# Order of the work inside a state-space tile, and B's diagonal blocks in two buffers

## The reference, cut to what matters

```python
dlt, Bm, Cm = split(u @ Wdbc.T)                  # u is (T, E)
delta = softplus(dlt @ Wdt.T + bdt)              # (T, E)
dA  = exp(delta[..., None] * A)                  # A = -exp(Alog), (E, N)
dBu = delta[..., None] * Bm[:, None, :] * u[..., None]
h_t = dA_t * h_(t-1) + dBu_t                     # scan over time, for each (e, n)
y_t = sum_n h_t[e, n] * C_t[n] + u_t * Dp
out = ((act_mx * (y of s=0)) + (act_mx * (y of s=1))) @ Wf.T + bf + skip
```

## Time and profile before

| what | value |
|---|---|
| median of 3 runs | 6061.12 us |
| the profiled execution, its own time | 6069.96 us |
| its span, first to last instruction | 6068.1 us |
| mean granted TensorE clock | 0.977 of full |
| state-space part, first scan to last | 3098.9 to 6014.5 us |
| busy: PE, DVE, ACT, POOL | 5548.3, 4367.1, 2989.3, 2960.3 us |

### The profile page before, as it was taken

One profiled execution on the slowest core, in us unless ns is written; L12 is line 12 of the kernel. 1 busy time (PEld: TensorE's weight loads), 2 busy tenths in 40 slices (PEclk: granted clock), 3 DMA queues, 4 the chain that ended last, 5 costly groups with the idle time before them and its releaser, 6 DMA issues. The chain is left out here.

```text
span 6068.1 us, 136615 instructions
## 1 busy us (share of the span) xinstructions
PE 5548.3 (91%) x58510; PEld 3145.8 (52%) x58510; DVE 4367.1 (72%) x5872; ACT 2989.3 (49%) x4999; POOL 2960.3 (49%) x955
## 2 busy tenths in 40 slices
PE   8899979997989899859989899999999999999998
PEld 3455545553555555434445555555555555555555
DVE  1455545552655555546559999999999999999996
ACT  0122212221555555531256666666666666666664
POOL 0000000000000000014359989999898998989997
PEclk9999989998999999979999999999999999999999
DMA  6200020001000000014331111111111111201111
GB/s 222 70 31 31 23 74 32 31 23 63 10 17 17 17 17 17 8 58 156 129 110 49 61 39 48 51 58 65 49 50 39 56 65 49 68 25 54 63 47 31
DMA packets 145197, 321.73 MB, mean 53 GB/s; under 512 B 25946, under 2 KB 27227, under 8 KB 134379
## 3 DMA queue, kind: packets, MB, share of 16 engines
q1 hardware_dynamic: 142322, 309.20, 14.8%
q10 hardware_dynamic: 2304, 4.20, 0.2%
HBM read 238.46 MB, written 74.89 MB: 52 GB/s over the span
## 5 line engine op out<-in xcount | busy, mean ns | idle before, releaser
L1896 POOL TENSOR_TENSOR sc_state<-sc_state,sc_c_rows 128x2048 f32<-128x2048 f32 x512 | 2374.2, 4642 | 288.6 <-DVE sc_state L2203 275.4
L2203 DVE TENSOR_TENSOR_SCAN sc_state<-sc_decay,wide 128x512 f32<-128x512 f32 x2048 | 2346.7, 1200 | 101.7 <-PE wide L2062 97.3
L1987 ACT ACTIVATE sc_decay<-sc_delta,sc_neg_a 128x512 f32<-128x512 f32 x2048 | 1455.6, 720 | 817.4 <-DVE sc_state L2203 804.7
L2062 PEld LDWEIGHTS wide<-sc_diag,sc_du_t 64*64 64x64 f32 x32768 | 972.6, 133 | 692.2 <-issue 455.8
L2062 PE MATMUL wide<-sc_diag,sc_du_t 64*64 64x128 f32 x32768 | 1173.4, 273 | 140.3 <-DVE sc_state L2203 140.3
L2079 PE MATMUL wide<-sc_state,sc_half 64*64 64x512 f32 x8192 | 1077.3, 592 | 10.4 <-POOL sc_state L1896 10.4
L1377 DVE CUSTOM_DVE_ANT_0 l_prob<-wide,l_mask_add 128x512 f32<-128x512 f32 x512 | 340.0, 683 | 285.9 <-PE wide L1247 285.7
L2036 PE MATMUL wide<-sc_xn_t,sc_w_z 128*128 128x512 f32 x1024 | 509.9, 621 | 2.5 <-DMA sc_xn_t<-xn_d 2.5
L1162 ACT ACTIVATE l_prob<-l_prob,l_s_max 128x512 f32<-128x512 f32 x512 | 366.0, 716 | 229.3 <-DVE l_s_max L1377 228.9
L509 PE MATMUL wide<-l_w,l_xn_t 128*128 128x512 f32 x1024 | 445.1, 592 | 1.7 <-PEq L84 1.7
L1258 PE MATMUL wide<-l_ident,l_prob 128*128 128x128 f32 x2048 | 293.9, 281 | 65.7 <-DVE l_prob_t L1386 38.6
(11 more groups left out here) (202 smaller groups left out, 6547.7 us busy)
## 6 DMA issues: line engine op xcount, KB each, us to landing
sc_c_rows<-c_d SPq DMA_DIRECT2D x64, 1024.0 KB, 4.8
sc_w_z<-wz_tiles SPq DMA_DIRECT2D x128, 256.0 KB, 2.7
x<-l_out SPq DMA_DIRECT2D x24, 1024.0 KB, 4.2
l_x<-x SPq DMA_DIRECT2D x16, 1024.0 KB, 6.4
mx_d<-fr_mx SPq DMA_DIRECT2D x16, 1024.0 KB
sc_mx<-mx_d SPq DMA_DIRECT2D x64, 256.0 KB, 2.7
pro_w_mod<-in_mod_w SPq DMA_DIRECT2D x6, 2048.0 KB, 11.3
l_w<-in_att_w SPq DMA_DIRECT2D x12, 1024.0 KB, 12.5
```

Of the source, the lines that this page charges most:

```text
L1896: pool.tensor_tensor(state[quad % STATES][:, :, :], state[quad % STATES][:, :, :], c_rows[(r * 4 + q) % ROWS][:, :, :], ALU.mult).then_inc ...
L1987: act.activation(decay[step % DECAYS][:, :], delta[slot % 2][:, :], ACT.Exp, scale=neg_a[:, s, m, n:n + 1]).then_inc(decay_ready, 1)
L2062: last = pe.matmul(to[cols_to, k, :, :], du_t[slot % 2][rows, k, cols_to], diag[rows, c, k, :, :], start=True, stop=True)
L2203: dve.tensor_tensor_scan(state[quad % STATES][:, step % 4, order], decay[step % DECAYS][:, order], pair[:, i, order], 0.0, ALU.mult, ALU.a ...
```

## The change

Within a slot, each engine's order is new. In odd chunks `inputs` takes the other half of the channels (`of`), so that the scans of the odd chunks run with the halves of the channels exchanged; for this ScalarE makes `delta_x`, delta with halves exchanged (`exchange`, two copies SBUF to SBUF at chunk 1 of each slot), the odd decays read it, and A is laid out to match on the host (`crossed`). `sums` then adds the even chunks' states to acc[0] straight and the odd chunks' to acc[1] crossed, which puts them right again. `swap_sums` and the tile `swap` are gone; the second add reads acc[1] in PSUM. `diag` has two buffers; GpSimd builds block m of the next set after quad 3 of slot m. C has 4 buffers in place of 5, z's weights 2 in place of 3; softplus runs a slot earlier.

```diff
@@ -1680,7 +1680,7 @@
     QUADS = SLOTS * 4
-    DECAYS, STATES, ROWS, WZ = 6, 4, 5, 3
+    DECAYS, STATES, ROWS, WZ = 6, 4, 4, 2
     AHEAD = DECAYS // 2
@@ -1703,7 +1703,7 @@
         b_tm = [sb(f"b_tm{i}", [P, 4, N]) for i in two]
-        diag = sb("diag", [P, 8, 4, 64, 2])
+        diag = [sb(f"diag{i}", [P, 8, 4, 64, 2]) for i in two]
         c_rows = [sb(f"c_rows{i}", [P, 4, T]) for i in range(ROWS)]
@@ -1712,7 +1712,7 @@
         y_sum = [sb(f"y_sum{i}", [P, ET, T]) for i in two]
-        swap = sb("swap", [P, T])
+        delta_x = sb("delta_x", [P, T])
         o_part = sb("o_part", [P, 256])
@@ -1735,7 +1735,7 @@
         decay_ready, dbu_full, scanned = sem("decay_ready"), sem("dbu_full"), sem("scanned")
-        weighted, summed, swapped = sem("weighted"), sem("summed"), sem("swapped")
+        weighted, summed, exchanged = sem("weighted"), sem("summed"), sem("exchanged")
         acc_drained, y_added, gated_ready = sem("acc_drained"), sem("y_added"), sem("gated_ready")
@@ -1792,7 +1792,6 @@
                 load_w(1)
-                load_w(2)
                 sp.dma_start(w_out[:, :, :], d["wfT"].rearrange("(k p) n -> p k n", p=P)).then_inc(w_out_loaded, 16)
@@ -1803,9 +1802,6 @@
                         load_set(r + 1)
-                        if r >= 1:
-                            sp.wait_ge(weighted, 4 * 8 * r)
-                        load_c(4 * (r + 1))
                     if slot + WZ < SLOTS:
@@ -1832,8 +1828,8 @@
                     if m == 7 and r + 1 < 2 * B:
-                        for q in range(1, 4):
-                            sp.wait_ge(weighted, 4 * slot + q)
+                        for q in range(4):
+                            sp.wait_ge(weighted, 4 * slot + q + 1)
                             load_c(4 * (r + 1) + q)
@@ -1858,9 +1854,9 @@
                         pool.wait_ge(b_loaded[r % 2], (r // 2 + 1) * 32)
-                    if r >= 1:
-                        pool.wait_ge(dbu_full, 4 * (64 * (r - 1) + 56 + c + 1))
-                    pool.tensor_tensor(diag[:, c, :, :, :],
+                    if r >= 2 and c == 0:
+                        pool.wait_ge(dbu_full, 4 * 64 * (r - 1))
+                    pool.tensor_tensor(diag[r % 2][:, c, :, :, :],
                                        b_tm[r % 2][:, :, 2 * c:2 * c + 2].unsqueeze(2).broadcast_to([P, 4, 64, 2]),
@@ -1895,10 +1891,9 @@
                                        c_rows[(r * 4 + q) % ROWS][:, :, :], ALU.mult).then_inc(weighted, 1)
-                    if m == 7 and r + 1 < 2 * B:
-                        build(r + 1, 2 * q)
-                        build(r + 1, 2 * q + 1)
-                    if q == 3 and slot >= 1 and where(slot - 1)[1] == 1:
+                    if q == 3 and r + 1 < 2 * B:
+                        build(r + 1, m)
+                    if q == 2 and slot >= 1 and where(slot - 1)[1] == 1:
                         gating(slot - 1)
@@ -1954,14 +1949,13 @@
 
-                def swap_sums(slot):
-
-                    act.wait_ge(summed, 16 * (slot + 1))
-                    if slot >= 1:
-                        act.wait_ge(y_added, slot)
+                def exchange(slot):
+
+                    act.wait_ge(decay_ready, 16 * slot + 2)
                     for g in range(2):
-                        act.activation(swap[g * 64:(g + 1) * 64, :], acc[1][(1 - g) * 64:(2 - g) * 64, :], ACT.Copy
-                                       ).then_inc(swapped, 1)
+                        act.activation(delta_x[g * 64:(g + 1) * 64, :], delta[slot % 2][(1 - g) * 64:(2 - g) * 64, :],
+                                       ACT.Copy).then_inc(exchanged, 1)
+                    act.wait_ge(exchanged, 2 * (slot + 1))
 
@@ -1973,33 +1967,38 @@
                 turned_du(0)
-                for chunk in range(CHUNKS + 8):
+                softplus(1)
+                softplus_end(1)
+                for chunk in range(CHUNKS + AHEAD):
+                    if chunk >= AHEAD:
+                        slot, c = (chunk - AHEAD) // 8, (chunk - AHEAD) % 8
+                        b, s, m = where(slot)
+                        if c == 5 and slot + 1 < SLOTS:
+                            turned_du(slot + 1)
+                        if c == 5 and b >= 1 and slot % 2 == 0:
+                            half_output((b - 1) * 2 * TT + slot % 16 // 2)
+                        if c == 7 and slot + 2 < SLOTS:
+                            softplus(slot + 2)
+                            softplus_end(slot + 2)
                     if chunk < CHUNKS:
...
                             act.wait_ge(delta_ready, slot + 1)
+                        if chunk % 8 == 1:
+                            exchange(slot)
+                        of = delta_x if chunk % 2 else delta[slot % 2]
                         for i in range(2):
...
                                 act.wait_ge(scanned, step - DECAYS + 1)
-                            act.activation(decay[step % DECAYS][:, :], delta[slot % 2][:, :], ACT.Exp,
+                            act.activation(decay[step % DECAYS][:, :], of[:, :], ACT.Exp,
                                            scale=neg_a[:, s, m, n:n + 1]).then_inc(decay_ready, 1)
-                    if chunk < AHEAD:
-                        continue
-                    slot, c = (chunk - AHEAD) // 8, (chunk - AHEAD) % 8
-                    b, s, m = where(slot)
-                    if c == 0 and slot + 1 < SLOTS:
-                        softplus(slot + 1)
-                        softplus_end(slot + 1)
-                    if c == 3 and slot >= 1:
-                        swap_sums(slot - 1)
-                    if c == 4 and slot + 1 < SLOTS:
-                        direct(slot + 1)
-                        turned_du(slot + 1)
-                    if c == 7 and b >= 1 and slot % 2 == 0 and slot < SLOTS:
-                        half_output((b - 1) * 2 * TT + slot % 16 // 2)
+                    if chunk >= AHEAD:
+                        slot, c = (chunk - AHEAD) // 8, (chunk - AHEAD) % 8
+                        if c == 2 and slot + 1 < SLOTS:
+                            direct(slot + 1)
 
@@ -2059,8 +2058,9 @@
                                 cols_to = slice(g * 64, (g + 1) * 64)
-                                last = pe.matmul(to[cols_to, k, :, :], du_t[slot % 2][rows, k, cols_to],
-                                                 diag[rows, c, k, :, :], start=True, stop=True)
+                                of = (g + c) % 2
+                                last = pe.matmul(to[cols_to, k, :, :], du_t[slot % 2][rows, k, of * 64:(of + 1) * 64],
+                                                 diag[r % 2][rows, c, k, :, :], start=True, stop=True)
                                 if k == 3:
@@ -2070,10 +2070,9 @@
                         if q == 0 and slot >= 1:
-                            pe.wait_ge(acc_drained, slot)
-                            pe.wait_ge(swapped, 2 * slot)
+                            pe.wait_ge(y_added, slot)
                     for i in range(2):
-                        n = 2 * h + i
+                        n = 2 * i + h
                         for g in range(2):
@@ -2103,24 +2102,27 @@
                     b, s, m = where(slot)
-                    if c <= 3 and slot >= 1:
-                        sums(4 * slot - 2 + c // 2, c % 2)
+                    if c in (0, 2) and slot >= 1:
+                        sums(4 * slot - 2, c // 2)
+                    if c == 3 and slot >= 1:
+                        sums(4 * slot - 1, 0)
+                        sums(4 * slot - 1, 1)
                     if slot == SLOTS:
                         continue
-                    if c in (0, 2) and slot + 1 < SLOTS:
-                        z_product(slot + 1, range(c, c + 2))
+                    if c == 1 and slot + 1 < SLOTS:
+                        z_product(slot + 1, range(DT))
                     if c == 4 and slot + 1 < SLOTS:
                         turn(slot + 1)
-                    if c == 5:
-                        sums(4 * slot, 0)
-                        sums(4 * slot, 1)
-                    if c >= 6:
-                        sums(4 * slot + 1, c - 6)
-                    if c == 6 and b >= 1:
+                    if c == 4 and b >= 1:
                         pe.wait_ge(z_direct, min(slot + 2, SLOTS))
                         output(b - 1, slot % 16 // 2, range(slot % 2 * 4, slot % 2 * 4 + 4))
-                    if c == 7 and slot + 2 < SLOTS:
+                    if c == 5 and slot + 2 < SLOTS:
                         dt_product(slot + 2)
+                    if c in (5, 6):
+                        sums(4 * slot, c - 5)
+                    if c == 7:
+                        sums(4 * slot + 1, 0)
+                        sums(4 * slot + 1, 1)
                 for piece in range(2 * TT):
@@ -2166,13 +2168,12 @@
 
-                def add_swapped(slot):
+                def add_others(slot):
 
...
                     y = y_sum[b % 2][:, m, :]
```

(27 more changed lines are left out.)

## The result

The changed kernel takes 5853.17 us (median of 4 runs, 5849.13 to 5855.86), the kernel before in the same group 6055.93: ratio 0.9659, 95% interval 0.9625 to 0.9693. In a later group of runs the changed kernel took 5851.41 and the kernel before 6070.25: 0.9641 (0.9628 to 0.9655). So it is 3.4 to 3.6% faster. The profiled execution took 5854.08 us against 6069.96 before, 215.9 us less.

The account below looks back on a forecast made before the run. TensorE was to bound the slots, VectorE the first batch element's: (22.93 - 21.45) x 110 = 163, plus 23, less 2.6 at the start, plus 0.7 at the end, 184 us less, giving 5878 us; range 5852 to 5962.

Parts of the forecast that it names:

- One sign: VectorE's scans, as a mark of a right forecast: they wait for TensorE once a slot, by 0.4 us, after z.
- TensorE's own work: TensorE's products in one slot, new order: inputs, sums, z, output, dt and turn sum to 21.38 us without waiting.
- 20.4 to 21.3: VectorE's work in one slot: scans, step size, scaled input, adds and drain, mean 20.9 us, below TensorE's.
- First batch element: Slots without output work: VectorE bounds them at 20.7 and 21.0 us, mean 20.85 against 22.28, 23 us less in all.
- the walk: One steady slot followed through TensorE and VectorE: TensorE waits nowhere over 0.07 us; z holds the scans 0.4 us a slot.
- The add from PSUM: VectorE's second add, reading PSUM: priced even with a free add from SBUF (0.67 us), its blocking behind GpSimd gone.
- +2.6: Kernel start: softplus(1) stands before the first decays and the first exchange follows, costing 2.6 us.
- The 0.7 at the end: Kernel end: no swap between the two adds, saving 0.7 us.
- A: Rival: only the add's blocking goes, turns at waiting stay; slots 22.57 and 21.3, about 6005 us; chance 0.14.
- B: Rival: GpSimd late for quad 2, stalling 28 output slots by 1 to 1.5 us; 42 us, so 5920; chance 0.12.
- C: Rival: blocks or operands late at the set's edge, or stalls move elsewhere; about no change, 6055 us; chance 0.04.
- D: Rival, slower: ScalarE's exchange and softplus make decays late, up to 3.6 us a slot, 6339 us; chance 0.04.

Follow-up runs that it names:

- z_halves: The changed kernel with z's product in two halves, in chunks 0 and 1, instead of one piece: 5901.51 us, ratio 0.9739 to the kernel before.
- only_diag: The kernel before with only diag's two buffers and one block of the next set built per slot: 6027.79 us, ratio 0.9929.
- cross_diag: The kernel before with crossed channels and spread blocks, but the old order on TensorE and ScalarE: 6054.20 us, ratio 0.9983.
- out_c6: The changed kernel with TensorE's output product back in chunk 6, leaving the turn alone in chunk 4: 5981.76 us, ratio 0.9858 to the kernel before.
- sbuf_add: The changed kernel with one diag buffer, blocks in each set's last slot, and the second add from an SBUF copy of acc[1]: 6108.79 us, ratio 1.0057.

## Why the prediction came out as it did

**Direction and mechanism right.** The slots shrank in the steady state (22.57 and 22.79 to 21.06 and 21.12), which is some 180 us of the 216, and the rest came from the ends of sets; TensorE's waits in chunk 4 are gone, the second add is at 0.66 everywhere, blocks are one a slot. One sign was half right: the scans wait for TensorE 52 times in 104 slots, by 0.34 us in the mean, and not once in each slot by 0.4.

**The step that failed: TensorE's own work, 21.38 us a slot, which I took with 0.07 of waiting as 21.45.** Measured where TensorE sets the length: 21.06. I had charged z as 2 x 1.91, "z twice 1.91", and output at 1.92, as the old order's rows had them, and counted only inputs' 0.06 to 0.11 for a change of shape. The rows after show 3.63 and 1.82: 0.29 us less, which leaves 21.09. The start of a group of 128-row products had its price inside each old row, and the new order has two such groups (z; turn with output) for four. z_halves bears this out: splitting z again puts 0.37 on the slot. Over 110 slots 21.45 - 21.14 = 0.31 is 34 us: 197 gained there, not 163. That is the whole miss between 184 and 216. (By its own numbers the sum gives 5877 as the median, 1 us below what was written.)

**VectorE.** The upper end of 20.4 to 21.3 was right: 21.28 with s = 1 and the drain, 20.95 without the drain where the same terms give 21.0. With TensorE at 21.06 it sets the slots with s = 1. The prediction had TensorE alone as the bound.

**First batch element:** 20.7 and 21.0 forecast, 20.72 and 20.95 measured; the walk held where VectorE sets the pace and z holds the scans.

**Ends of sets:** all their excess is gone. only_diag shows that some 40 us could be had by the spread blocks alone, in the old order; in the new one they are worth 30.

**The add from PSUM** was priced even: 664 ns mean against 669. The Trainium skill's fixed costs ("VectorE: DVE Perf Modes", the section on the trn2 errata), by which the prediction estimated PSUM to be 65 ns dearer, are not borne out for this add. The prediction gave the end of the add's holding a value only at the ends of sets. That was right for the kernel before, where slots with a held add are no longer than the others, but it did not see that in the new order an add from SBUF would have cost 226 us.

**Start and end:** +2.6 was forecast; z's scaled input comes 1.23 earlier than before and slot 0's add 1.57 later, so +2.8. That the two agree is in part luck: VectorE now also waits 1.01 us for z at the start (before 3108.46), which the sum had not, and no longer waits twice 0.56 for softplus. The 0.7 at the end did not show: the distance from slot 125's add to the end is 81.72, before 81.65.

**Rivals.** A (turns at waiting stay) fell for the changed kernel; cross_diag, with everything but the order, keeps the turns at waiting as A had it, but at slots of 22.80 and 6054 us where A had 22.57 and 6005. B (GpSimd late for quad 2) is true in small: two of the four slots with an output step in each batch element are 0.3 us longer (21.6 and 21.38 for 21.28 and 21.07), 12 x 0.3 = 4 us in all. The prediction had 0.5 us to spare there with products of 4.50; they take 4.57. C and D did not occur; the exchange's copies took 629 ns, between the bounds.

## What to carry to other kernels

When two engines are each busy nearly all the time and still wait, walk one period with both of their orders: freeing one of them of a wait (here the second add's, by the crossing alone) was worth nothing until the order let it count. Group TensorE's products by shape, and price a group, not a product: one more group of 128-row products among 64x64 ones cost 0.37 us in z_halves and 0.30 in out_c6. Before moving a step on one engine, list which tiles it frees and who overwrites them next; a step one quad later cost 7 us a time through such a wait.

## What the hardware showed that was not expected

- A VectorE add with two SBUF inputs that meets a running GpSimd product waits for its end: 2434 ns median in sbuf_add against 664 from PSUM, up to 6187. It is not let in between two products that follow each other without a gap: in the rows of sbuf_add it begins at 4588.07, the first of the two products is over near 4588.7, and the add ends with the second; before the change it began at 4566.39, when the first of three products in a row was over, and sat through the rest of the second and all of the third. The reverse is seen too: a product that begins just after such an add ends about 0.5 us late (9.59 for two in place of 9.08).
- z's eight records of 128x512 took 3.63 us in one group and 2 x 1.91 in two, and slots grew by 0.37: that is the price of one more group, with the granted clock at 1.00 of full from 3500 to 5700 us in z_halves and in the changed kernel.
